# Ones as a sixteen-column denominator beside each head's values, division in the stage that follows each attention

## The chip, the cores and the metric

The kernel runs on one core of one Trainium2 chip. The metric is the device time of one execution, in microseconds (us). A core has a matrix engine (PE, with PEld for its weight loads), a vector engine (DVE), a scalar engine (ACT), a general one (POOL), and SP, which here only issues transfers (DMAs). Each engine runs its own list of instructions in order, and they wait for each other through semaphores; transfers run on 16 DMA engines.

## The reference

Eight batches of 512 tokens, 256 wide, go through a transformer layer with 16 heads of 16 columns each:

```
x = x + xattn(layernorm(x), ctx)                # 1601 context rows, 16 heads, softmax
g = layernorm(x)
h = g + causal_self_attention(rmsnorm(g)*g1)    # rotary, 16 heads of 16
y = h + moe(rmsnorm(h)*g2)                      # 8 experts, top 2
x = x + y
```

Both attentions compute, per head and query, `sum_k exp(s_k - max) v_k / sum_k exp(s_k - max)`. The change concerns only how the sum in the denominator is produced, stored and divided by.

## The kernel before, in words

`build` (from L1917) runs stages one after the other, each closed by a barrier of all engines (`Prog.clear`, L62): weights, projections of the inputs, cross attention, `invert_denominators` (L841), `project_self` (L887), self attention, `invert_denominators` again, `finish_self` (L1150), routing, experts, combination.

**attention (L442).** The work is 32 units, one for each batch and group of four heads (GH = 4). In a unit PE computes the scores of a tile of 128 keys with 512 queries (`scores`, L649), ACT takes the exponential, and PE multiplies values by probabilities into one bank `ps_o` of 128 rows (`products`, L661). Each head owns VW = 32 columns of the weights `va`: 16 values, one column of ones, 15 of zeros. So of the 32 rows of `ps_o` that a head owns, 16 are numerators, one is the denominator and 15 are zero. ACT copies the bank to `ob` (`take_out`, L808), and SP stores it (`send_out`, L587) as one transfer of 128 rows of 512 numbers, 256 KB.

SP's list in one unit u (`unit`, L591) is: wait until PE has finished the last products of unit u-1; load the values of unit u+1 (cross) or u+3 (self), in 8 or 4 transfers; load keys and queries of unit u+3 in 12 transfers (`load_kq`); wait for `take_out` of unit u-1; store it. PE first needs the keys and queries of unit u+3 at step 5 of the 16 steps of unit u+1 (self), when the row maxima for that unit begin (`in_order`, L534). POOL's part at the start of each attention is the memsets of `va`.

**invert_denominators.** SP gathers the 128 denominator rows (one for each unit and head) into a 128x512 tile, DVE takes the reciprocal, SP stores it; then a barrier.

**load_attention_out (L865).** SP loads, for one batch, the numerators in four transfers of 128 KB into `oT` (128 x 2 x 512) and the inverses in two transfers of 256 KB, each inverse row repeated over 16 partitions, into `inv`.

**project_self and finish_self.** Both work batch by batch in turns (`turns`, L137): in one turn every engine runs its parts for several batches, the lag saying how many batches behind. In `project_self` DVE's list in turn t is: `subtract_high` of k (batch t-3), `residual` (t-1), `divide` (t), `rope` of q (t-2), `layer_norm` (t-1), `rms_inverse` (t-1), `subtract_high` of q (t-2), `rope` of k (t-2). PE's is: `turn_rows` (t-1), `out_product` (t), `q_products`, `v_product`, `k_products` (t-1). The k products wait until DVE has read the q products (`rope_read`). SP's is: wait for `divide` (t-1), load batch t, then stores of k, v, rows and q. `residual` waits for the stores of the rows of the batch before (`rows_sent`). In `finish_self` DVE's list is `residual` (t-1), `divide` (t), `mean_square`, `rms_inverse`, logits; SP loads the rows of batch t-1 and the attention output of batch t.

Of the kernel before, what the change touches and what calls it, by code (L numbers as in the profile page):

```python
# [8 lines left out]
ALU = mybir.AluOpType  # L9
# [3 lines left out]
P = 128  # L13
DIM = 256
KC = DIM // P
HEADS = 16
HD = DIM // HEADS
GH = 4
# [423 lines left out]
def attention(nc, q_parts, k_parts, v_rows, out_rows, kv, causal, keep, units, beside=None):  # L442
# [28 lines left out]
    with ExitStack() as stack:  # L471
# [30 lines left out]
        KQ = 16 * 2 * PAIRS  # L502
        VLOADS = 16 * GH * ((1 if kv >= P else 0) + (1 if kv % P else 0))
# [60 lines left out]
        with nc.Block() as block:  # L564
            @block.sync
            def _(sp):
# [36 lines left out]
                for k in range(2):  # L603
                    sp.sem_inc(o_sent[k], 16)
# [11 lines left out]
                for k in range(2):  # L616
                    sp.wait_ge(o_sent[k], 16 * (units // 2 + 1))

            @block.tensor
            def _(pe):  # L620
# [71 lines left out]
                pe.wait_ge(ones_set, BUFS + 2 * VBUFS + 1)  # L692
# [43 lines left out]
            def _(pool):  # L736
# [7 lines left out]
                pool.wait_ge(ones_set, BUFS + 2 * VBUFS)  # L744
                nc.gpsimd.memset(nm_parts[:, 3:, :], 0.0).then_inc(ones_set, 1)
                pool.wait_ge(ones_set, BUFS + 2 * VBUFS + 1)
# [35 lines left out]
            def _(act):  # L782
# [25 lines left out]
                def take_out(u):  # L808
                    act.wait_ge(pv_done, (u.n + 1) * STEPS + RING)
                    act.wait_ge(o_sent[u.odd], u.loads(2) * 16)  # L810
                    nc.scalar.copy(ob[u.odd][:, :], ps_o[:, :]).then_inc(o_read, 1)
# [26 lines left out]
def invert_denominators(nc, out_rows, inverse, own, units):  # L838

    n = units * GH  # L840
    with ExitStack() as stack:  # L841
        p = Prog(nc, stack, "inv_self_" if own else "inv_cross_")
        den = p.sb("den", [n, SEQ])
        inv = p.sb("inv", [n, SEQ])
        den_in = p.sem("den_in")
        inv_ready = p.sem("inv_ready")
        inv_sent = p.sem("inv_sent")
        with nc.Block() as block:
            @block.sync
            def _(sp):  # L850
                src = out_rows.rearrange("u (j w) n -> u j w n", w=VW)[:, :, HD, :].rearrange("u j n -> (u j) n")
                sp.dma_start(den[:, :], src).then_inc(den_in, 16)
                sp.wait_ge(inv_ready, 1)
                sp.dma_start(inverse, inv[:, :]).then_inc(inv_sent, 16)
                sp.wait_ge(inv_sent, 16)

            @block.vector
            def _(dve):
                dve.wait_ge(den_in, 16)
                nc.vector.reciprocal(inv[:, :], den[:, :]).then_inc(inv_ready, 1)  # L860
        p.clear()
# [15 lines left out]
ATT_LOADS = 16 * (GROUPS + KC)  # L877

def project_self(nc, x_in, out_rows, inverse, x1_rows, h0_rows, q_parts, k_parts, v_rows, keep, batches):


    with ExitStack() as stack:
        p = Prog(nc, stack, "slf_")
        oT = p.sb("oT", [P, KC, SEQ])
        inv = p.sb("inv_rows", [P, KC, SEQ])  # L887
# [20 lines left out]
        on_ready = p.sem("on_ready")  # L908
        xb_ready = p.sem("xb_ready")
# [26 lines left out]
        with nc.Block() as block:  # L936
            @block.sync
            def _(sp):
                def load(b):
                    sp.wait_ge(on_ready, b + 1)  # L940
                    load_attention_out(sp, out_rows, inverse, oT, inv, b, att_in)
# [84 lines left out]
            def _(dve):  # L1026
# [123 lines left out]
def finish_self(nc, out_rows, inverse, x1_rows, h0_rows, y_rows, hn_rows, keep, batches):  # L1150

    logits = keep["logits"]
    with ExitStack() as stack:
        p = Prog(nc, stack, "fin_")
        oT = p.sb("oT", [P, KC, SEQ])
        inv = p.sb("inv_rows", [P, KC, SEQ])
# [14 lines left out]
        on_ready = p.sem("on_ready")  # L1171
        o_done = p.sem("o_done")
# [14 lines left out]
        with nc.Block() as block:  # L1187
            @block.sync
            def _(sp):
                def load_attention(b):  # L1190
                    sp.wait_ge(on_ready, b + 1)
                    load_attention_out(sp, out_rows, inverse, oT, inv, b, att_in)
# [41 lines left out]
            def _(dve):  # L1234
# [3 lines left out]
                def divide(b):  # L1238
                    dve.wait_ge(att_in, (b + 1) * ATT_LOADS)
                    nc.vector.tensor_tensor(on[:, :, :], oT[:, :, :], inv[:, :, :], ALU.mult).then_inc(on_ready, 1)  # L1240
# [687 lines left out]
def build(nc, a, out, batches=8):  # L1928
# [6 lines left out]
    out_rows = dram("out_rows", [units, P, SEQ])  # L1935
    inverse = dram("inverse", [units * GH, SEQ])
# [3 lines left out]
    out2_rows = dram("out2_rows", [units, P, SEQ])  # L1940
    inverse2 = dram("inverse2", [units * GH, SEQ])
# [8 lines left out]
    with ExitStack() as stack:  # L1950
# [15 lines left out]
        with ExitStack() as zeros_stack:  # L1966
            z, beside = zeros_beside(nc, in_sorted, zeros_stack, tiles, units)
            attention(nc, q_parts, k_parts, v_rows, out_rows, CTX, False, keep, units, beside)
            z.clear()
        invert_denominators(nc, out_rows, inverse, False, units)  # L1970
        project_self(nc, a["x"], out_rows, inverse, x1_rows, h0_rows, q2_parts, k2_parts, v2_rows, keep, batches)
        beside = gate_up_beside(nc, a, keep, p, units)
        attention(nc, q2_parts, k2_parts, v2_rows, out2_rows, SEQ, True, keep, units, beside)
        invert_denominators(nc, out2_rows, inverse2, True, units)
# [4 lines left out]
        finish_self(nc, out2_rows, inverse2, x1_rows, h0_rows, y_rows, hn_rows, keep, batches)  # L1979
# [32 lines left out]
```

## Time and profile before

| | us |
|---|---|
| median of 3 runs | 3300.74 (3298.10 to 3301.28) |
| the profiled execution's own time | 3297.82 |
| its span | 3296.2 |
| PE busy | 2698.5 (82%) |
| DVE busy | 1763.2 (53%) |
| ACT busy | 1458.2 (44%) |
| POOL busy | 490.7 (15%) |

Busy shares are averages over stages with different limits. The stages' places in the span, from the starts of their first instructions: cross attention to 1660, first inversion 1661 to 1670, `project_self` 1670 to 1903, self attention 1903 to 2296, second inversion 2297 to 2306, `finish_self` from 2306. In a row of the timeline the first number is the start in us from the span's start, the second the time from the start of the first instruction in the row to the end of its last, then engine (SPq and ACTq are the issuing of a DMA), line, operation, output and inputs, shapes and count, and in brackets the idle time before and what ended it.

### The profile page before, as it was taken

Reading aid. Unit: us, or ns where it says so; the run is one execution under the profiler, and the core shown is the slowest. Engines: PE = TensorE matmul, PEld = TensorE weight load, DVE = VectorE, ACT = ScalarE, POOL = GpSimd, SP = SyncE. Lnnn points to the kernel's source line nnn. Section 1 sums busy time; section 2 is a strip of 40 time slices with the busy share of each in tenths; the row PEclk is TensorE's granted clock in tenths of the full one; section 3 lists DMA queues with packets and bytes.
Section 4 is the critical chain, followed back from the end, with each engine's and each line's share of the span. In section 5 each row is a group of like instructions: output and inputs, shape, how many; then the busy total and the mean of one; then the engine's idle time right before and its main releaser. Section 6 shows DMA issues by size and latency. Waiting matters only on the chain. (4 is left out here: it accounts for less than half of the span.)

```text
span 3296.2 us, 55561 instructions
## 1 busy us (share of the span) xinstructions
PE 2698.5 (82%) x14654; PEld 1323.0 (40%) x14655; DVE 1763.2 (53%) x2832; ACT 1458.2 (44%) x2927; POOL 490.7 (15%) x650
## 2 busy tenths in 40 slices
PE   7996999999999999999949879887340299999980
PEld 5662232323232323233225434443340177777760
DVE  4565876767676767677436656664222022222223
ACT  2331576767676767677723336565010022222210
POOL 2444000000000000000014421110223300000006
PEclk9996899999999999999979979999665699999995
DMA  6777544444454444454035456653444211100116
GB/s 211 215 233 133 70 62 67 62 66 63 62 64 62 63 63 63 62 63 61 17 115 185 159 121 133 133 133 102 149 150 155 84 32 32 32 32 32 32 47 183
DMA packets 524784, 313.32 MB, mean 95 GB/s; under 512 B 312112, under 2 KB 486848, under 8 KB 524480
## 3 DMA queue, kind: packets, MB, share of 16 engines
q1 hardware_dynamic: 492752, 256.93, 38.6%
q0 software_dynamic: 11392, 37.76, 3.5%
q10 hardware_dynamic: 20464, 16.40, 1.6%
q8 instruction: 96, 1.57, 0.2%
q14 instruction: 80, 0.66, 0.1%
HBM read 188.91 MB, written 121.26 MB: 94 GB/s over the span
## 5 line engine op out<-in xcount | busy, mean ns | idle before, releaser
L719 DVE TENSOR_REDUCE att_cross_neg_max<-att_cross_ps_s 128x1 f32<-128x802 f32 x1024 | 965.6, 988 | 350.9 <-PE att_cross_ps_s L636 349.2
L794 ACT ACTIVATE att_cross_probs<-att_cross_ps_st 128x512 f32<-128x512 f32 (+1 forms) x1664 | 901.2, 599 | 394.7 <-PE att_cross_ps_st L655 382.2
L655 PE MATMUL att_cross_ps_st<-att_cross_q_pack,att_cross_k_pack 99*128 99x512 bf16 (+1 forms) x1664 | 575.0, 391 | 37.3 <-issue 28.4
L636 PE MATMUL att_cross_ps_s<-att_cross_k_pack,att_cross_q_pack 96*128 96x401 bf16 x2048 | 547.9, 350 | 70.1 <-DVE att_cross_neg_max L719 29.5
L670 PE MATMUL att_cross_ps_o<-att_cross_probs,att_cross_v_tiles 128*32 128x512 f32 (+1 forms) x3328 | 453.5, 618 | 1.0
L636 PEld LDWEIGHTS att_cross_ps_s<-att_cross_k_pack,att_cross_q_pack 96*128 96x128 bf16 x2048 | 176.8, 100 | 420.5 <-DVE att_cross_neg_max L719 204.9
L655 PEld LDWEIGHTS att_cross_ps_st<-att_cross_q_pack,att_cross_k_pack 99*128 99x128 bf16 (+1 forms) x1664 | 163.1, 100 | 415.5 <-ACT att_cross_probs L794 293.2
L719 DVE TENSOR_REDUCE att_self_neg_max<-att_self_ps_s 128x1 f32<-128x128 f32 (+3 forms) x512 | 236.2, 489 | 148.7 <-PE att_self_ps_s L639 145.7
L794 ACT ACTIVATE att_self_probs<-att_self_ps_st 128x256 f32<-128x256 f32 (+3 forms) x512 | 208.2, 441 | 142.4 <-PE att_self_ps_st L658 136.6
L1744 DVE COPY moe_hiddenT<-moe_ps_h 128x256 f32<-128x256 f32 x142 | 60.3, 425 | 296.9 <-PE moe_ps_h L1654 296.9
L636 PE MATMUL att_self_ps_s<-att_self_k_pack,att_self_q_pack 96*128 96x128 bf16 (+3 forms) x512 | 158.7, 312 | 56.4 <-DMA att_self_q_pack<-q_parts 25.1
L1708 ACT ACTIVATE moe_silu<-moe_ps_g 128x352 f32<-128x352 f32 x142 | 65.8, 463 | 301.0 <-PE moe_ps_u L1646 301.0
L1664 PE MATMUL moe_ps_y<-top_wd_sb,moe_hiddenT 128*128 (+1 forms) x852 | 196.0, 379 | 1.1 <-DVE moe_hiddenT L1745 1.1
L1646 PE MATMUL moe_ps_g<-top_wg_sb,moe_rowsT 128*128 x568 | 192.8, 462 | 0.0
L1646 PE MATMUL moe_ps_u<-top_wu_sb,moe_rowsT 128*128 x568 | 192.0, 461 | 0.0
L765 POOL CAST att_cross_neg_max_parts<-att_cross_neg_max_merged 128x16 bf16<-128x16 f32 x32 | 6.1, 192 | 1236.9 <-DVE att_cross_neg_max_merged L710 1236.9
L1664 PEld LDWEIGHTS moe_ps_y<-top_wd_sb,moe_hiddenT 128*128 128x128 f32 (+1 forms) x852 | 161.7, 190 | 35.1 <-issue 1.4
L655 PE MATMUL att_self_ps_st<-att_self_q_pack,att_self_k_pack 99*128 99x256 bf16 (+3 forms) x512 | 154.8, 304 | 7.7 <-DMA att_self_q_pack<-att_self_neg_max_rows 6.5
L1738 DVE TENSOR_TENSOR moe_hidden<-moe_ps_u,moe_silu 128x352 f32<-128x352 f32 x142 | 73.5, 517 | 159.2 <-ACT moe_silu L1708 159.2
L1816 POOL DMA_INDIRECT comb_row<-out_sorted,comb_index x64 | 61.9, 968 | 622.5 <-DVE comb_index L1826 603.3
L1646 PEld LDWEIGHTS moe_ps_u<-top_wu_sb,moe_rowsT 128*128 128x128 f32 x568 | 108.5, 191 | 60.7 <-issue 1.0
L670 PEld LDWEIGHTS att_cross_ps_o<-att_cross_probs,att_cross_v_tiles 128*32 128x32 f32 (+1 forms) x3328 | 66.6, 109 | 151.5 <-ACT att_cross_probs L794 113.8
(208 smaller groups left out, 2901.7 us busy)
## 6 DMA issues: line engine op xcount, KB each, us to landing
att_cross_k_pack<-k_parts SPq DMA_DIRECT2D x192, 200.1 KB, 7.5
k_parts<-in_part SPq DMA_DIRECT2D x72, 256.0 KB, 3.1
in_rows<-in_ctx_dram SPq DMA_DIRECT2D x24, 512.0 KB, 4.4
v_rows<-in_v_biased SPq DMA_DIRECT2D x24, 512.0 KB, 2.9
att_cross_q_pack<-q_parts SPq DMA_DIRECT2D x192, 64.0 KB, 7.7
att_cross_v_tiles<-v_rows SPq DMA_DIRECT2D x128, 96.0 KB
att_self_k_pack<-k_parts SPq DMA_DIRECT2D x192, 64.0 KB, 3.1
att_self_q_pack<-q_parts SPq DMA_DIRECT2D x192, 64.0 KB, 3.1
```

Source lines behind the costliest of these rows:

```text
L636: last = nc.tensor.matmul(ps_s[bank][:, n, 0:w], qp[v.buf][0:SROWS, j, q * P:(q + 1) * P], kp[v.buf][0:SROWS, j, s:s + w], start=True, sto ...
L655: mm = nc.tensor.matmul(ps_st[bank_of_step[s]][0:rows, q0:SEQ], kp[u.buf][0:MROWS, j, t * P:t * P + rows], qp[u.buf][0:MROWS, j, q0:SEQ], ...
L670: nc.tensor.matmul(ps_o[j * VW:(j + 1) * VW, q0:SEQ], va[u.vbuf][0:rows, t, j, :], pr[0:rows, (u.odd * STEPS + t * GH + j) % RING, q0:SEQ] ...
L719: nc.vector.tensor_reduce(nmax[v.odd][:, col, half:half + 1], ps_s[bank][:, 0:len(spans), 0:spans[0][1]], AX.XY, ALU.max, negate=True).the ...
L765: link(nc.gpsimd.tensor_copy(nm_parts[:, 0, :], full))
L794: nc.scalar.activation(pr[0:rows, (u.odd * STEPS + s) % RING, q0:SEQ], ps_st[bank_of_step[s]][0:rows, q0:SEQ], ACT.Exp).then_inc(exp_done, 1)
L1646: last = nc.tensor.matmul(ps[half][:, 0:HHALF], xT[t.par][:, i, :], wt[:, bass.ds(at, HHALF)], start=(i == 0), stop=(i == KC - 1))
L1664: last = nc.tensor.matmul(ps_y[:, :], hT[half][0:CW[c], c, :], wd[0:CW[c], bass.ds(at, DIM)], start=(half == 0 and c == 0), stop=(half == ...
L1708: nc.scalar.activation(sil[half][:, :], ps_g[half][:, 0:HHALF], ACT.Silu).then_inc(sil_ready, 1)
L1738: nc.vector.tensor_tensor(h[half][:, :], ps_u[half][:, 0:HHALF], sil[half][:, :], ALU.mult)\
L1744: nc.vector.tensor_copy(hT[half][:, 0:CH - 1, :], ps_h[half][:, 0:CH - 1, :])
L1816: pool.indirect_dma_start(out=r[g][k][c][:, :], out_offset=None, in_=out_sorted, in_offset=bass.IndirectOffsetOnAxis(ap=index[g][:, c, k:k ...
```

## The change

`va` gets 16 columns of ones instead of one of ones and 15 of zeros, so each head owns 16 numerator rows and 16 equal denominator rows. `send_out` stores them in eight transfers of 16 rows (32 KB) instead of one of 128 rows (256 KB): four to `out_rows` and four to `den_rows`, both now [batch, 256, 512]. Both calls of `invert_denominators` and the stage itself are gone. `load_attention_out` loads one batch with two transfers of 512 KB. `divide` in both stages takes the reciprocal of the whole 128x1024 tile of denominators in place, waits for it, and multiplies.

```diff
 def send_out(v):
     sp.wait_ge(o_read, v.n + 2)
-    sp.dma_start(out_rows[v.n, :, :], ob[v.odd][:, :]).then_inc(o_sent[v.odd], 16)
+    for rows, first in ((out_rows, 0), (den_rows, HD)):
+        for j in range(GH):
+            sp.dma_start(rows[v.batch, v.rows.start + j * HD:v.rows.start + (j + 1) * HD, :],
+                         ob[v.odd][j * VW + first:j * VW + first + HD, :]).then_inc(o_sent[v.odd], 16)
...
 for k in range(VBUFS):
-    nc.gpsimd.memset(va[k][:, :, :, HD + 1:VW], 0.0).then_inc(ones_set, 1)
-    nc.gpsimd.memset(va[k][:, :, :, HD:HD + 1], 1.0).then_inc(ones_set, 1)
+    nc.gpsimd.memset(va[k][:, :, :, HD:VW], 1.0).then_inc(ones_set, 1)
...
-def load_attention_out(eng, out_rows, inverse, oT, inv, b, arrived):
-
-    for c in range(KC):
-        for u in range(GROUPS // KC):
-            src = out_rows[b * GROUPS + (c * (GROUPS // KC) + u), :, :].rearrange("(j w) n -> j w n", w=VW)
-            eng.dma_start(oT[u * GR:(u + 1) * GR, c, :], src[:, 0:HD, :]).then_inc(arrived, 16)
-        heads = HEADS // KC
-        src = inverse[bass.ds(b * HEADS + c * heads, heads), :].unsqueeze(1).broadcast_to([heads, HD, SEQ])
-        eng.dma_start(inv[:, c, :], src).then_inc(arrived, 16)
+def load_attention_out(eng, out_rows, den_rows, oT, den, b, arrived):
+
+    for src, dst in ((out_rows, oT), (den_rows, den)):
+        eng.dma_start(dst[:, :, :], src[b, :, :].rearrange("(c p) n -> p c n", p=P)).then_inc(arrived, 16)
...
 def divide(b):
     dve.wait_ge(att_in, (b + 1) * ATT_LOADS)
-    nc.vector.tensor_tensor(on[:, :, :], oT[:, :, :], inv[:, :, :], ALU.mult).then_inc(on_ready, 1)
+    nc.vector.reciprocal(den[:, :, :], den[:, :, :]).then_inc(inverted, 1)
+    dve.wait_ge(inverted, b + 1)
+    nc.vector.tensor_tensor(on[:, :, :], oT[:, :, :], den[:, :, :], ALU.mult).then_inc(on_ready, 1)
...
-invert_denominators(nc, out_rows, inverse, False, units)
...
-invert_denominators(nc, out2_rows, inverse2, True, units)
```

SP's list in one self attention unit, from the last loads of keys and queries over the store of the output to the values of the next unit (ISA and REGISTER_ALU rows are address and wait instructions). Before:

```order
L572 DMA att_self_q_pack<-q_parts 16x4x512
L588 REGISTER_ALU
L589 ISA [waits att_self_o_read]
L589 DMA out_rows<-att_self_out_buf 128x512
L594 ISA
L580 ISA [waits att_self_pv_done]
L580 DMA att_self_v_tiles<-v_rows 128x4x16
```

And now:

```order
L573 DMA att_self_q_pack<-q_parts 16x4x512
L589 REGISTER_ALU
L592 ISA [waits att_self_o_read]
L592 DMA out_rows<-att_self_out_buf 16x512
L592 ISA
L592 DMA out_rows<-att_self_out_buf 16x512
L592 ISA
L592 DMA out_rows<-att_self_out_buf 16x512
L592 ISA
L592 DMA out_rows<-att_self_out_buf 16x512
L592 DMA den_rows<-att_self_out_buf 16x512 x4
L598 ISA
```

Seven more transfers stand between the queries of one unit and the values of the next.

DVE's list in one turn of `project_self`, from the moments of the residual to the q rope. Before:

```order
L176 BN_AGGR slf_norm_mean_var<-slf_norm_stats 128x2 x4
L1031 REGISTER_ALU
L1032 TENSOR_TENSOR slf_o_normed<-slf_oT,slf_inv_rows 128x1024 [waits slf_att_in]
L1059 ISA
L1060 REGISTER_ALU [waits slf_rope_done]
L1062 TENSOR_TENSOR slf_rope_cos<-slf_ps_a,top_keep_constants 128x512 [waits slf_full_ready0]
```

And now:

```order
L176 BN_AGGR slf_norm_mean_var<-slf_norm_stats 128x2 x4
L1002 REGISTER_ALU
L1003 RECIPROCAL slf_denominators<-slf_denominators 128x1024 [waits slf_att_in]
L1005 TENSOR_TENSOR slf_o_normed<-slf_oT,slf_denominators 128x1024 [waits slf_inverted]
L1032 ISA
L1033 REGISTER_ALU [waits slf_rope_done]
L1035 TENSOR_TENSOR slf_rope_cos<-slf_ps_a,top_keep_constants 128x512 [waits slf_full_ready0]
```

A reciprocal of 1024 columns stands ahead of the multiplication, and with it ahead of everything that DVE does later in the turn.

## Rows read from the trace of the kernel before

**Rows 1.** Windows: length, busy us (count) PE, PEld, DVE, ACT, POOL; clock, DMA, GB/s.
```profile
1700.00:1860.00 160.00, 148.11 (x491) 88.88 (x492) 107.99 (x240) 54.92 (x87) 73.07 (x49) 0.98 0.54 177
1934.00:2292.00 358.00, 322.34 (x3021) 154.85 (x3017) 220.72 (x479) 219.14 (x567) 42.25 (x154) 1.00 0.57 128
2305.00:2460.00 155.00, 65.05 (x272) 54.73 (x272) 38.77 (x97) 21.14 (x42) 35.17 (x31) 0.66 0.48 153
```

**Rows 2.** Timeline from the first inversion stage to the first division of project_self.
```profile
1660.96 0.34 SPq L852 DMA_DIRECT2D inv_cross_den<-out_rows  x1
1663.63 3.35 DVE L860 RECIPROCAL inv_cross_inv<-inv_cross_den 128x512 f32<-128x512 f32 x1 [50.27 <-DMA inv_cross_den<-out_rows]
...
1670.02 1.30 SPq L871 DMA_DIRECT2D slf_oT<-out_rows  x2
...
1681.54 1.22 DVE L1032 TENSOR_TENSOR slf_o_normed<-slf_oT,slf_inv_rows 128x1024 f32<-128x1024 f32 x1 [14.56 <-DMA slf_inv_rows<-inverse]
```

**Rows 3.** Instructions on one tile: L1044, duration ns min/median/max.
```profile
L1044 DVE RECIPROCAL slf_norm_std_inv<-slf_norm_std x8: 159/168/171, 1695.5 to 1858.3; 128x4 f32<-128x4 f32 x8
```

**Rows 4.** DMA issues of the page: count, KB each, median us to landing.
```profile
fin_x<-x_rows SPq DMA_DIRECT2D x8, 512.0 KB, 4.6
fin_h<-h_rows SPq DMA_DIRECT2D x8, 512.0 KB, 6.8
```

**Rows 5.** Timeline of DVE and PE in project_self, turns 1 to 3.
```profile
1694.32 1.23 DVE L1032 TENSOR_TENSOR slf_o_normed<-slf_oT,slf_inv_rows 128x1024 f32<-128x1024 f32 x1 [2.82 <-DMA slf_inv_rows<-inverse]
...
1712.31 1.22 DVE L1038 TENSOR_TENSOR slf_x<-slf_ps_o,slf_x_biased 128x1024 f32<-128x1024 f32 x1 [10.37 <-DMA h_rows<-slf_h]
...
1734.13 1.23 DVE L1070 TENSOR_TENSOR slf_roped_rest<-slf_roped,slf_roped_part 128x1024 f32<-128x1024 f32 x1 [4.59 <-ACT slf_roped_part L1113]
...
1738.36 1.19 DVE L1032 TENSOR_TENSOR slf_o_normed<-slf_oT,slf_inv_rows 128x1024 f32<-128x1024 f32 x1
...
1745.76 3.60 PE L1003 MATMUL slf_ps_b<-slf_xT,top_keep_wk_rot 128*128 128x512 f32 x8
...
1750.60 1.09 PE L994 MATMUL slf_ps_t<-top_keep_constants,slf_x_rms 128*128 128x128 f32 x8 [1.25 <-ACT slf_x_rms L1095]
```

**Rows 6.** Clock: a window of finish_self, and sixteen equal matmuls in project_self (timeline).
```profile
2321.00:2327.00 6.00, 5.48 (x16) 4.18 (x16) 0.42 (x2) 0.00 (x0) 0.00 (x0) 0.69 0.27 84
...
1728.55 3.62 PE L985 MATMUL slf_ps_o<-top_keep_WoT,slf_o_normed 128*128 128x256 f32 x16
```

**Rows 7.** Timeline of SP and PE in two self attention units; landing of the queries.
```profile
2057.94 2.09 SPq L580 DMA_DIRECT2D att_self_v_tiles<-v_rows  x4
2060.22 0.35 SPq L569 DMA_DIRECT2D att_self_k_pack<-k_parts  x1
...
2065.70 0.38 SPq L572 DMA_DIRECT2D att_self_q_pack<-q_parts  x1
...
2069.19 2.06 SPq L580 DMA_DIRECT2D att_self_v_tiles<-v_rows  x4
...
2069.58 0.22 PE L636 MATMUL att_self_ps_s<-att_self_k_pack,att_self_q_pack 96*128 96x128 bf16 x1
...
att_self_q_pack<-q_parts SPq DMA_DIRECT2D x192, 64.0 KB, 3.1
```

**Rows 8.** SP's waits in the two attentions: us in total, times, longest us.
```profile
SPq L580 <- PE att_self_ps_o L670: 65.3, 28, 8.0
...
SPq L580 <- PE att_cross_ps_o L670: 907.2, 30, 43.2
```

**Rows 9.** Timeline: the second inversion stage and the first load of finish_self.
```profile
2296.82 0.35 SPq L852 DMA_DIRECT2D inv_self_den<-out_rows  x1
...
2305.66 1.28 SPq L871 DMA_DIRECT2D fin_oT<-out_rows  x2
```

**Rows 10.** Timeline: first and last of the eight divisions in finish_self.
```profile
2319.79 1.22 DVE L1240 TENSOR_TENSOR fin_o_normed<-fin_oT,fin_inv_rows 128x1024 f32<-128x1024 f32 x1 [17.00 <-DMA fin_inv_rows<-inverse]
...
2445.78 1.23 DVE L1240 TENSOR_TENSOR fin_o_normed<-fin_oT,fin_inv_rows 128x1024 f32<-128x1024 f32 x1 [5.94 <-DMA fin_inv_rows<-inverse]
```

More of the change, by code:

```diff
@@ L438, in project_inputs, with attention @@
         p.clear()
-def attention(nc, q_parts, k_parts, v_rows, out_rows, kv, causal, keep, units, beside=None):
+def attention(nc, q_parts, k_parts, v_rows, out_rows, den_rows, kv, causal, keep, units, beside=None):
     tiles = [(t, min(P, kv - t * P)) for t in range(-(-kv // P))]
@@ L616, in _ @@
                 for k in range(2):
-                    sp.wait_ge(o_sent[k], 16 * (units // 2 + 1))
+                    sp.wait_ge(o_sent[k], OSENT * (units // 2 + 1))
             @block.tensor
@@ L809, in take_out @@
                     act.wait_ge(pv_done, (u.n + 1) * STEPS + RING)
-                    act.wait_ge(o_sent[u.odd], u.loads(2) * 16)
+                    act.wait_ge(o_sent[u.odd], u.loads(2) * OSENT)
                     nc.scalar.copy(ob[u.odd][:, :], ps_o[:, :]).then_inc(o_read, 1)
@@ L834, in attention, with project_self @@
         p.clear()
[L838 to L861, printed above, removed]
-def load_attention_out(eng, out_rows, inverse, oT, inv, b, arrived):
-    for c in range(KC):
-        for u in range(GROUPS // KC):
-            src = out_rows[b * GROUPS + (c * (GROUPS // KC) + u), :, :].rearrange("(j w) n -> j w n", w=VW)
-            eng.dma_start(oT[u * GR:(u + 1) * GR, c, :], src[:, 0:HD, :]).then_inc(arrived, 16)
-        heads = HEADS // KC
-        src = inverse[bass.ds(b * HEADS + c * heads, heads), :].unsqueeze(1).broadcast_to([heads, HD, SEQ])
-        eng.dma_start(inv[:, c, :], src).then_inc(arrived, 16)
-ATT_LOADS = 16 * (GROUPS + KC)
-def project_self(nc, x_in, out_rows, inverse, x1_rows, h0_rows, q_parts, k_parts, v_rows, keep, batches):
+def load_attention_out(eng, out_rows, den_rows, oT, den, b, arrived):
+    for src, dst in ((out_rows, oT), (den_rows, den)):
+        eng.dma_start(dst[:, :, :], src[b, :, :].rearrange("(c p) n -> p c n", p=P)).then_inc(arrived, 16)
+ATT_LOADS = 16 * 2
+def project_self(nc, x_in, out_rows, den_rows, x1_rows, h0_rows, q_parts, k_parts, v_rows, keep, batches):
     with ExitStack() as stack:
@@ L1146, in project_self, with finish_self @@
         p.clear()
-def finish_self(nc, out_rows, inverse, x1_rows, h0_rows, y_rows, hn_rows, keep, batches):
+def finish_self(nc, out_rows, den_rows, x1_rows, h0_rows, y_rows, hn_rows, keep, batches):
     logits = keep["logits"]
@@ L1934, in build @@
     v_rows = dram("v_rows", [batches, CTX, DIM])
-    out_rows = dram("out_rows", [units, P, SEQ])
-    inverse = dram("inverse", [units * GH, SEQ])
+    out_rows = dram("out_rows", [batches, DIM, SEQ])
+    den_rows = dram("den_rows", [batches, DIM, SEQ])
     k2_parts = dram("k2_parts", [batches, 3, DIM, SEQ], BF16)
@@ L1939, in build @@
     v2_rows = dram("v2_rows", [batches, SEQ, DIM])
-    out2_rows = dram("out2_rows", [units, P, SEQ])
-    inverse2 = dram("inverse2", [units * GH, SEQ])
+    out2_rows = dram("out2_rows", [batches, DIM, SEQ])
+    den2_rows = dram("den2_rows", [batches, DIM, SEQ])
     tokens = batches * SEQ
@@ L1967, in build @@
             z, beside = zeros_beside(nc, in_sorted, zeros_stack, tiles, units)
-            attention(nc, q_parts, k_parts, v_rows, out_rows, CTX, False, keep, units, beside)
+            attention(nc, q_parts, k_parts, v_rows, out_rows, den_rows, CTX, False, keep, units, beside)
             z.clear()
-        invert_denominators(nc, out_rows, inverse, False, units)
-        project_self(nc, a["x"], out_rows, inverse, x1_rows, h0_rows, q2_parts, k2_parts, v2_rows, keep, batches)
+        project_self(nc, a["x"], out_rows, den_rows, x1_rows, h0_rows, q2_parts, k2_parts, v2_rows, keep, batches)
         beside = gate_up_beside(nc, a, keep, p, units)
-        attention(nc, q2_parts, k2_parts, v2_rows, out2_rows, SEQ, True, keep, units, beside)
-        invert_denominators(nc, out2_rows, inverse2, True, units)
+        attention(nc, q2_parts, k2_parts, v2_rows, out2_rows, den2_rows, SEQ, True, keep, units, beside)
         keep["logits"] = p.sb("logits", [P, tokens // P, EXPERTS])
@@ L1978, in build @@
         keep["tile_expert"] = p.sb("tile_expert", [P, tiles], I32)
-        finish_self(nc, out2_rows, inverse2, x1_rows, h0_rows, y_rows, hn_rows, keep, batches)
+        finish_self(nc, out2_rows, den2_rows, x1_rows, h0_rows, y_rows, hn_rows, keep, batches)
         route(nc, keep, tokens)
```

23 lines of the change are left out of this document (14 added, 9 removed).

## The prediction

> **What bounds the kernel now.** I read the windows first, cut at the stages that the change touches. In `project_self` PE is busy 148 of 160 us and DVE 108; in self attention PE 322 of 358; in `finish_self` nobody is busy for half the time [rows 1]. A busy share doesn't say whether an added microsecond shows, so in each stage I look for the wait that ends last.
>
> In `project_self` that is a ring through DVE's list. In a steady turn DVE starts `subtract_high` of k at 1734.13 after waiting 4.59 us for ACT, which waited for POOL, which waited for what DVE did at the end of the turn before. From there DVE runs residual, moments, division (1738.36), rope, layer norm without a gap [rows 5]. PE's k products wait for the rope of q, end at 1749.36 (1745.76 + 3.60), and 1.24 us later `turn_rows` begins, waiting for ACT's scaled rows, again from DVE [rows 5]. Whatever is put between residual and rope lengthens the ring. In self attention PE sets the pace, but SP is close behind: it waits for PE only 65.3 us in 28 units, 2.33 us in each [rows 8]. In `finish_self` the division waits for its loads in every turn [rows 10].
>
> **What is removed.** The two inversion stages: 1660.96 to 1670.02, or 9.06 us, and 2296.82 to 2305.66, or 8.84 us [rows 2, 9]. Both lie bare between barriers, so both go in full.
>
> **Price of a reciprocal.** 128x512 took 3.352 us (3.35 in [rows 2]) and 128x4 0.168 us [rows 3]: 6.27 ns a column, 0.14 us fixed. For 1024 columns 6.56 us. Doubling the first row gives 6.70, the 1.19 us of a 1024-column multiplication [rows 5] is the floor; I take 6.56, since it follows the operation's own two sizes. There are now 8 of them in each stage.
>
> **Price of the stores.** Each unit has seven more issues on SP. Twelve key and query issues of 32 or 64 KB start from 2060.22 to 2065.70, 0.50 us apart [rows 7]; the four value issues take 2.09 us. Seven at 0.50 us are 3.5 us a unit. The lower end is 7 x 0.35 (an issue's own duration), 2.5 us, the upper 7 x 0.56 (the values' spacing), 3.9 us.
>
> **Cross attention: nothing.** SP waits 907.2 us there [rows 8], more than 28 us a unit, and covers 3.5. Values of one instead of zero leave the matmuls' shapes alone, and the memsets get fewer. If this cover were gone it would be 32 x 3.5 us; nothing suggests it.
>
> **End of cross attention to the first division.** The last store is bare: +3.5. The inversion goes: -9.06. The load took 11.52 us from first issue to division (1670.02 to 1681.54) [rows 2]. The new one is two transfers of 512 KB; a pair of that size and form lands 6.8 us after the second is issued, some 7.4 after the first [rows 4]. The same bytes in the old form give 11.52 as the upper end; I take 7.4, the row of the same shape: -4.1. The reciprocal is bare: +6.56. Together -3.1.
> The Trainium skill, on its page "DMA: Bandwidth & Descriptors" (section "Why a DMA increments its semaphore by 16 and not by 1"), says that a transfer is split over the largest number of engines, up to 16, that divides the outermost dimension on both sides. By that the old numerator loads (outermost 4) would use 4 of 16 engines and the new ones all; if it didn't hold, the loads would take their old times and the sum would be 4.1 + 6.7 + 7 x 5.4 = 49 us higher.
>
> **project_self, turn 1.** The division had waited 2.82 us for its load [rows 5]; it waits no more, so the reciprocal costs 6.56 - 2.8 = +3.8. The residual of the next turn waited 10.37 us for the rows' store [rows 5], queued behind the loads that get 4 us shorter, and PE's product was ready about 2.5 us before it: of 3.8, +1.3 is left.
>
> **project_self, turns 2 to 7.** Each takes 6.56 in full, since DVE has no gap between residual and rope and the ring closes through both rope and layer norm. The steady residual waits up to 0.58 us for the stores, 0.3 on average, which vanishes. The k products can now start only about 6 us after the v products end, so PE stands idle once a turn. After such a gap the granted clock in `finish_self` is 0.69 on average, between the 1.2 GHz level and the 2.4 GHz one, and 16 matmuls take 5.48 us, where they take 3.62 in `project_self` at 2.4 GHz [rows 6]: 1.9 us more for a burst, of which 1.24 is slack, so +0.6. A turn costs 6.56 - 0.3 + 0.6 = 6.9; six turns +41.4. The stage with its boundary comes to -3.1 + 1.3 + 41.4 = **+39.6**.
>
> **Self attention.** SP's unit gets 3.5 us longer and has 2.33 us to give [rows 8]. Is there a reserve in how early it loads? The last queries of a unit are issued at 2065.70 and land 3.1 us later, at 2068.8; PE uses them at 2069.58 [rows 7]. So 0.8 us, once. From the second or third unit on PE waits for keys and queries, and the unit's period becomes SP's: 3.5 - 2.33 = 1.17 us longer. Over 27 units **+31.6**. With 2.5 us for the issues it is about +4, with 3.9 about +42. What is queued behind SP's issues are the very loads that PE waits for; ACT's `take_out` waits for a store two units old and is not reached first.
>
> **Second boundary.** +3.5 for the last store, -8.84, load 14.13 (2305.66 to 2319.79 [rows 9, 10]) to 7.4: -6.7, reciprocal +6.56. Together **-5.5**.
>
> **finish_self, turns 1 to 7.** Divisions are 126.0 us apart over seven turns, 18.0 each [rows 10]. Each waits for its load, and the next load is issued when it is done, so a shorter load pays and the reciprocal costs. The two first loads took 11.5 and 14.1 us, 12.8 on average; against 7.4 that saves 5.4. 6.56 - 5.4 = 1.2 a turn, **+8.4**. The ends are -0.1 (saving of 6.7) and 6.56 (no saving): -1 to +46.
>
> **Sum.** 39.6 + 31.6 - 5.5 + 8.4 = +74.1. The profiled execution took 3297.8 us, so 3371.9; the median of the runs shown lies 2.9 higher, which gives **3375 us**.
>
> **Rivals.**
> A. *SP keeps up.* The issues go out at their own duration, and PE hardly waits: self attention costs some 4 us instead of 32. 3375 - 28 = 3347. For it: issue rows of 0.35 to 0.38 us; against it: in steady loops the starts are 0.50 apart. Chance 15%.
> B. *The final stage pays for each reciprocal.* The load's speed is not what ends its turn, because transfers of other tensors hold it: +46 instead of +8, 3413. For it: other loads and stores share each turn; against it: those transfers can use the reciprocal's time. Chance 11%.
> C. *The clock.* After the idle gap the k products, 7.2 us at 2.4 GHz, run wholly at 1.2 GHz: 7.2 more, less 1.24 of slack, 6.0 instead of 0.6 in six turns, +32, 3407. For it: that gap is new in every turn. Against it: after idle stretches in `finish_self` a burst lost 1.9 us, not its whole length [rows 6]. Chance 4%.
> The Trainium skill's page "TensorE: Matmul & The Clock Gate" (section "HAM oscillation — how this bites in real kernels") has the rule behind this: a wait in every tile drops the clock each time, and the next tile starts slow. The windows agree as far as 0.69 against 1.00 goes.
> D. *Faster.* The reciprocals vanish in DVE's idle time, and the removed stages are a net gain. In `project_self` DVE is idle 52 us of 160 [rows 1] and eight reciprocals are 52.5 us; `finish_self` has 116 idle. Then the sum is -9.06 - 8.84 + 7.0 - 4.1 - 6.7 = -21.7, 3279, provided SP keeps up too. It decides if a turn of `project_self` is set by PE alone, with DVE's 4.59 us wait being true slack. Against it: that wait is the ring's own. Chance 4%.
> The other 66% are the forecast.
>
> **How the numbers follow.** The range takes the bounds of the stores' price (3347 to 3386), and reaches up to B and C: 3340 to 3415. Below it lie D and the cheaper half of A, above it B and C with dear stores; about 2 in 10. A measurement can tell 0.2%, 6.6 us, from no change. Faster is D, 0.04; A together with free reloads in the final stage could come near zero only if `project_self` paid little, 0.02; slower 0.94.
>
> **What would show it.** `project_self`: turns of 30 us instead of 23.4, an idle PE of some 6 us before the k products, reciprocals of 6.5 to 6.6 us. Self attention: waits of PE for DMA of keys and queries, SP's wait for PE near zero, units of 12.3 us. `finish_self`: first division near 15 us after the first issue, turns near 19. No inversion rows. It is wrong if SP still waits 2 us a unit, if turns of `project_self` grow by less than 5 us, or if loads of 512 KB land as slowly as the old ones.

## The result, and the profile after

The median after the change is **3332.49 us** (4 runs, 3329.0 to 3333.01) against 3300.15 us before (4 runs of the same comparison): a ratio of 1.0096, 95% interval 1.0079 to 1.0114, so 1% slower. The profiled execution took 3329.0 us, its span is 3327.4 us (before 3296.2): 31.2 us more. The forecast was 74 us more, and 3332.49 lies below the range of 3340 to 3415: the direction was right, the size wrong.

Cut at the same instructions, the two spans compare so. The stages are: `project_self` from its first attention load to the first key load of self attention; self attention from there to the last `take_out`; then the boundary to the first load of `finish_self`; `finish_self` to the first memset of routing.

| us | before | after | difference | forecast |
|---|---|---|---|---|
| first load of `project_self` at | 1670.0 | 1664.3 | -5.7 | -5.6 |
| `project_self` | 233.6 | 276.5 | +42.9 | +45.2 |
| self attention | 388.6 | 416.0 | +27.4 | +31.6 |
| second boundary | 13.5 | 7.9 | -5.6 | -5.3 |
| `finish_self` | 177.1 | 151.1 | **-25.9** | **+8.3** |
| the rest of the program | 813.5 | 811.6 | -1.9 | 0 |

Five lines hold within 5 us. One has the wrong sign, and it alone makes up 34 of the 43 us by which the forecast was off.

The end of the first boundary and the first division of `project_self` after the change (timeline; answers to [rows 2]):

```profile
1658.27 1.81 SPq L592 DMA_DIRECT2D den_rows<-att_cross_out_buf  x4
...
1664.27 0.40 SPq L844 DMA_DIRECT2D slf_oT<-out_rows  x1
1664.72 0.46 SPq L844 DMA_DIRECT2D slf_denominators<-den_rows  x1
...
1669.33 6.55 DVE L1003 RECIPROCAL slf_denominators<-slf_denominators 128x1024 f32<-128x1024 f32 x1 [56.13 <-DMA slf_denominators<-den_rows]
```

No inversion stands there, and the reciprocal takes 6.55 us as priced from the 128x512 and the 128x4 one (6.56). But the load is there 5.06 us after its first issue (before 11.52, forecast 7.4). One steady turn of `project_self` (timeline of DVE and PE, turns 4 and 5; answers to [rows 5]):

```profile
1770.13 6.52 DVE L1003 RECIPROCAL slf_denominators<-slf_denominators 128x1024 f32<-128x1024 f32 x1
1770.71 3.62 PE L988 MATMUL slf_ps_t<-top_keep_wv,slf_xT 128*128 128x256 f32 x16
...
1780.36 5.95 PE L974 MATMUL slf_ps_a<-slf_xT,top_keep_wk 128*128 128x512 f32 x8 [6.03 <-DVE slf_rope_sin L1036]
...
1786.14 3.60 PE L974 MATMUL slf_ps_b<-slf_xT,top_keep_wk_rot 128*128 128x512 f32 x8
...
1789.58 1.04 PE L965 MATMUL slf_ps_t<-top_keep_constants,slf_x_rms 128*128 128x128 f32 x8
...
1795.96 1.23 DVE L1043 TENSOR_TENSOR slf_roped_rest<-slf_roped,slf_roped_part 128x1024 f32<-128x1024 f32 x1 [3.70 <-ACT slf_roped_part L1086]
...
1800.18 6.52 DVE L1003 RECIPROCAL slf_denominators<-slf_denominators 128x1024 f32<-128x1024 f32 x1
```

The turn is 30.05 us (1770.13 to 1800.18), with DVE's 3.70 us wait for ACT still in it, so the ring is the one of before with a link more. PE stands idle 6.03 us before the k products, and the first eight of them take 5.95 us instead of 3.60.

SP in a self attention unit, and the waits of the stage from its first unit on (timeline, then waits: who for whom, us in total, times, longest; answers to [rows 7, 8]):

```profile
2105.01 1.88 SPq L592 DMA_DIRECT2D out_rows<-att_self_out_buf  x4
2106.98 1.76 SPq L592 DMA_DIRECT2D den_rows<-att_self_out_buf  x4
2109.02 2.22 SPq L581 DMA_DIRECT2D att_self_v_tiles<-v_rows  x4
...
SPq L581 <- PE att_self_ps_o L674: 8.1, 1, 8.1
...
PE att_self_ps_s L640 <- DMA att_self_q_pack<-q_parts: 30.4, 22, 2.8
```

The next unit's value loads start at 2121.39, 12.37 us after these: SP issues without a pause. It waits for PE once, where it waited 28 times, and PE now waits for queries 22 times, 30.4 us in all.

The first turns of `finish_self` after the change, the last division, and its transfers (timeline, then DMA issues with us to landing; answers to [rows 9, 10, 4]):

```profile
2364.68 0.41 SPq L844 DMA_DIRECT2D fin_oT<-out_rows  x1
...
2370.00 6.55 DVE L1214 RECIPROCAL fin_denominators<-fin_denominators 128x1024 f32<-128x1024 f32 x1 [27.16 <-DMA fin_denominators<-den_rows]
...
2392.78 5.25 PE L1184 MATMUL fin_ps_o<-top_keep_wo,fin_o_normed 128*128 128x256 f32 x16 [9.04 <-DVE fin_o_normed L1216]
...
2398.06 1.23 DVE L1223 TENSOR_TENSOR fin_h<-fin_ps_o,fin_h 128x1024 f32<-128x1024 f32 x1 [2.54 <-PE fin_ps_o L1184]
2399.20 6.54 DVE L1214 RECIPROCAL fin_denominators<-fin_denominators 128x1024 f32<-128x1024 f32 x1
...
2477.76 6.55 DVE L1214 RECIPROCAL fin_denominators<-fin_denominators 128x1024 f32<-128x1024 f32 x1
...
fin_oT<-out_rows SPq DMA_DIRECT2D x8, 512.0 KB, 4.2
fin_denominators<-den_rows SPq DMA_DIRECT2D x8, 512.0 KB, 5.1
hn_rows<-fin_h_normed ACTq DMA_DIRECT2D x8, 512.0 KB, 4.8
```

The first load takes 5.3 us (before 14.1). The later ones are there 5.3 to 7.4 us after their first issue, and DVE comes for them 6.3 to 7.9 us after it: of the later reciprocals only the seventh waits for its load, 0.90 us. A turn is (2477.76 - 2370.00) / 7 = 15.4 us, where it was 18.0 and 19.2 was forecast. The store of the normalised rows lands after 4.8 us, before after 8.9, though nothing of that store was edited.

So the questions are: do the eight stores make self attention longer, and through SP (E1)? What does a reciprocal cost in each stage (E2, E3)? What makes the loads fast (E4, E5, E7, E9)? What holds a turn of `finish_self` (E10, E11)?

### The profile page after: what moved, and what is told of

The parts are those of the page before. It is cut to its first block and busy times, and to the rows that moved or that the text cites. A ratio compares the mean times of both kernels' runs of the same rounds, so it can differ in the third digit from the quotient of the medians.

```text
span 3327.4 us, 56360 instructions
## 1 busy us (share of the span) xinstructions
PE 2721.3 (82%) x14654; PEld 1331.6 (40%) x14655; DVE 1860.1 (56%) x2846; ACT 1461.7 (44%) x2927; POOL 486.7 (15%) x644
```

## The experiments

Times of stages are read as in the table above. A time without an interval is that of one execution, to be compared with the 3329.0 us of the change's profiled one. The runs were taken in four groups, each with the kernel before beside it, and its median differed from group to group: 3300.15 us beside the change, 3303.07 beside E1 to E4, 3293.07 beside E5 and E7 to E9, 3300.92 beside E10 and E11. What lies behind `finish_self`, which no edit touches, took 811.6 to 813.6 us in the first two groups, 805.2 to 808.2 in the third, 814.6 to 814.9 in the fourth. So whole times of two groups can lie up to 10 us apart without any edit, and the argument goes by the stages.

### E1. One store instead of eight

```diff
-    for rows, first in ((out_rows, 0), (den_rows, HD)):
-        for j in range(GH): ...
+    sp.dma_start(out_rows[v.n, :, :], ob[v.odd][:, :]).then_inc(o_sent[v.odd], 16)
...
+    src = out_rows[bass.ds(b * GROUPS + c * 2, 2), :, :]
+    src = src.rearrange("u (j w) n -> (u j) w n", w=VW)[:, first:first + HD, :]
+    eng.dma_start(dst[:, c, :], src).then_inc(arrived, 16)
```

> One store of 128 rows a unit again instead of eight of 16, and the loads in four transfers of 256 KB (8 heads of 16 rows each) because the rows lie as before. Theory (SP's issues delay the loads of keys and queries): the self attention stage falls from 416.6 us back to 389, its unit from 12.37 to 11.1, SP waits over 2 us a unit again; each boundary loses 3 us. Span 3327 - 27 - 6 = 3294, up to 10 more if four loads land later than two. Rival (the denominator rows' extra lines or the memory written, not the number of issues, slow the stage): self attention stays at 416, span about 3321.

Self attention fell from 416.0 to 391.9 us, and SP waits for PE as before the change (waits of E1):

```profile
SPq L581 <- PE att_self_ps_o L671: 69.8, 28, 8.3
```

So the seven added issues are what lengthens self attention: 24 of the 27 us go with them. It isn't the memory written, for E1 writes the same 256 KB in a unit. Yet the whole took 3335.21 us (2 runs; ratio 1.0098, interval 1.0069 to 1.0127), no better than the change, because the loads that have to pick their rows out of the mixed store are slow again. First load of `finish_self` (timeline of E1):

```profile
2340.65 1.38 SPq L844 DMA_DIRECT2D fin_oT<-out_rows  x2
2342.09 1.24 SPq L844 DMA_DIRECT2D fin_denominators<-out_rows  x2
...
2350.90 6.55 DVE L1214 RECIPROCAL fin_denominators<-fin_denominators 128x1024 f32<-128x1024 f32 x1 [28.55 <-DMA fin_denominators<-out_rows]
```

10.2 us instead of 5.3; the turn is 19.0 us and `finish_self` 180.3. I had expected the form of these four loads to cost little and a span of 3294 to 3304 us; it was 3334.6.

### E2 and E3. No reciprocal in one of the stages

```diff
 def divide(b):
     dve.wait_ge(att_in, (b + 1) * ATT_LOADS)
-    nc.vector.reciprocal(den[:, :, :], den[:, :, :]).then_inc(inverted, 1)
-    dve.wait_ge(inverted, b + 1)
     nc.vector.tensor_tensor(on[:, :, :], oT[:, :, :], den[:, :, :], ALU.mult).then_inc(on_ready, 1)
```

E2 leaves this out in `project_self`, E3 in `finish_self`; each multiplies by the denominators there instead of dividing by them.

> The changed kernel without the reciprocal in project_self (it multiplies by the denominators; what it computes is not the reference). Theory (the reciprocal lies bare in DVE's ring, and the idle gap of PE costs some 0.5 us a turn): turns fall from 30.0 to 23.3, the first division comes 6.5 us earlier, stage -50, span 3277. Rival (the ring grew for another reason, such as the denser loads colliding with stores): turns stay above 25, span above 3290.

> The changed kernel without the reciprocal in finish_self (not the reference's computation). Theory (a turn of 15.4 us is product, residual, reciprocal, multiplication in a row, with the load of 5 us hidden beside product and residual): the turn falls until the chain of stores and loads over two turns sets it, 11 to 12 us; with the first reciprocal -34, span 3293. If nothing else binds, 8.5 us a turn and span 3273. Rival (a turn is set by the transfers' total of 3 MB): turn stays above 14, span above 3310.

E2 took 3278.2 us: `project_self` 276.5 to 223.1, 53.4 us for eight reciprocals of 6.55 us, 52.4 in all. The stage pays for them in full, though not evenly: the seven turns get 3.9 to 7.6 us shorter. Its steady turn is 22.96 us (multiplications at 1746.58 and 1769.55), against 30.05 and more, so with the colder k products a reciprocal costs 7.1 us in a steady turn.

E3 took 3320.3 us: `finish_self` 151.1 to 142.0, only 9.1 us for the same 52.4. The divisions, eight of them from 2370.2 to 2469.7, lie 14.2 us apart, just 1.2 less than with the reciprocal. I had expected 11 to 12 us and a span of 3293; the rival noted there, a turn above 14 us and a span above 3310, came true, and E10 below shows what holds that turn. What fills the rest of the turn there (timeline of E3, fourth and fifth turn):

```profile
2418.60 1.22 DVE L1220 TENSOR_TENSOR fin_h<-fin_ps_o,fin_h 128x1024 f32<-128x1024 f32 x1 [10.27 <-DMA fin_h<-h_rows]
...
2422.08 1.77 DVE L1213 TENSOR_TENSOR fin_o_normed<-fin_oT,fin_denominators 128x1024 f32<-128x1024 f32 x1 [2.26 <-DMA fin_denominators<-den_rows]
```

Without the reciprocal DVE waits for transfers of other tensors. SP too issues the next attention load late, 3.6 to 7.5 us after the multiplication in five of seven turns, because its loads of rows stand first and wait for POOL. With the reciprocal that time passes under it: SP then issues 0.16 to 0.27 us after every multiplication.

### E4 and E5. The form of the loads

E4 is E1 with the numerators and denominators loaded in the old form, eight transfers of 128 KB with four heads outermost. E5 keeps the dense stores and loads them in eight transfers of 128 KB too, but with 32 rows outermost.

```diff
 E4:
+    src = out_rows[b * GROUPS + c * 2 + u, :, :].rearrange("(j w) n -> j w n", w=VW)
+    eng.dma_start(dst[u * GR:(u + 1) * GR, c, :], src[:, first:first + HD, :]).then_inc(arrived, 16)
 E5:
+    for i in range(4):
+        eng.dma_start(dst[i * 32:(i + 1) * 32, :, :],
+                      src[b, :, :].rearrange("(c p) n -> p c n", p=P)[i * 32:(i + 1) * 32, :, :]).then_inc(arrived, 16)
```

> One store a unit as in the run with one store, and the loads in the old form: eight transfers of 128 KB whose source has four heads as its outermost dimension. Theory (the form makes the old loads slow, since few DMA engines serve one): the first load of finish_self takes 11 to 14 us instead of 5.3, the turn 20 to 22 instead of 15.4; self attention 389; span 3294 + 8 + 50 = about 3350. Rival (bytes and total traffic decide, not the form): first load near 6 to 8, turn 16 to 17, span below 3310.

> The changed kernel with each load of a batch cut into four pieces of 32 partitions: eight transfers of 128 KB, as many and as large as in the run with the old form (first load of finish_self 15.4 us, stage 222 us), but 32 as their outermost dimension instead of 4. Theory (the form, through the number of engines that serve a transfer): first load 7 to 8 us, 5.3 plus the longer issue; finish_self from first load to routing 151 to 158 us, span 3328 to 3338. Rival (number and size of the transfers): first load near 15 us, stage near 222, span near 3398.

First loads of `finish_self` (timeline of E4, then of E5):

```profile
2358.23 2.43 SPq L844 DMA_DIRECT2D fin_oT<-out_rows  x4
2360.70 2.34 SPq L844 DMA_DIRECT2D fin_denominators<-out_rows  x4
...
2373.65 6.55 DVE L1214 RECIPROCAL fin_denominators<-fin_denominators 128x1024 f32<-128x1024 f32 x1 [33.74 <-DMA fin_denominators<-out_rows]
```

```profile
2367.50 1.75 SPq L845 DMA_DIRECT2D fin_oT<-out_rows  x4
2369.29 1.84 SPq L845 DMA_DIRECT2D fin_denominators<-den_rows  x4
...
2373.93 6.55 DVE L1217 RECIPROCAL fin_denominators<-fin_denominators 128x1024 f32<-128x1024 f32 x1 [27.75 <-DMA fin_denominators<-den_rows]
```

The same 1 MB in the same number of transfers: 15.4 us in the one form, 6.4 in the other. E4 took 3395.4 us, with 303.5 us in `project_self` and 222.1 in `finish_self`, where a turn is 24.2 us; that is dearer than I had expected. E5 took 3338.5 us; against the change `finish_self` is 10.0 us longer (161.2) and `project_self` 2.9. So number and size of the transfers cost something, 16.8 us a turn instead of 15.4, but they are not what makes the old loads slow. E4 and E5 differ in the stores as well; E1 and E9 below have the same store and four loads of 256 KB each, with 8 and with 16 outermost, and take 10.2 and 6.9 us.

### E7. The kernel before, with sixteen outermost

If that is so, the kernel before can have fast loads without new stores, inversions kept: numerators and inverses are loaded with the 16 columns of a head outermost. The rows of `oT` then come in another order (column, then head), so the rows of both output weights are permuted once to fit.

```diff
-        for u in range(GROUPS // KC): ...
+        src = out_rows[bass.ds(b * GROUPS + c * (GROUPS // KC), GROUPS // KC), :, :]
+        src = src.rearrange("u (j w) n -> w (u j) n", w=VW)[0:HD, :, :]
+        eng.dma_start(oT[:, c, :], src).then_inc(arrived, 16)
...
-        src = inverse[...].unsqueeze(1).broadcast_to([heads, HD, SEQ])
+        src = inverse[...].unsqueeze(0).broadcast_to([HD, heads, SEQ])
```

> The kernel before, inversion stages and single store kept, but the order of a head's rows and the heads is swapped within a chunk of 128 (Wo's rows follow), so that each of the four loads of a batch, 256 KB, has 16 as outermost dimension. Theory (faster loads alone are worth 10 us in project_self and 35 us in finish_self, which the changed kernel had and lost again to the reciprocals and stores): stages 223 and 142 us, span 3296 - 45 = 3251. Rival (the gain in finish_self came with the denser order of the whole change, not with the loads): finish_self stays above 165 us, span above 3280.

3251.67 us median of 4 runs, ratio to the kernel before 0.9871 (0.9854 to 0.9887): 1.3% faster. `finish_self` takes 143.1 us instead of 177.1, self attention 387.3 and `project_self` 227.0. First load of `finish_self` (timeline of E7):

```profile
2300.37 0.63 SPq L885 DMA_DIRECT2D fin_oT<-out_rows  x1
...
2307.28 1.23 DVE L1254 TENSOR_TENSOR fin_o_normed<-fin_oT,fin_inv_rows 128x1024 f32<-128x1024 f32 x1 [10.21 <-DMA fin_inv_rows<-inverse]
```

6.9 us instead of 14.1. The turn is (2405.2 - 2307.3) / 7 = 14.0 us instead of 18.0. So 4.0 us a turn is what fast loads give by themselves, with no reciprocal in the stage and no other store of the attention in play.

### E8. The reciprocal at another place of DVE's turn

```diff
-turns(dve, batches, ((3, lambda b: subtract_high(1, b)), (1, residual), (0, divide), ...
+turns(dve, batches, ((0, invert), (3, lambda b: subtract_high(1, b)), (1, residual), (0, divide), ...
```

The reciprocal of `project_self` is put at the start of the turn, where DVE waited for ACT; `divide` keeps the multiplication.

> The changed kernel with the reciprocal of project_self as the first item of DVE's turn, ahead of the wait for ACT, the multiplication left in its place. Theory (the reciprocal is bare only where it stands; DVE has 4.9 us of waiting at the start of a turn): a turn falls from 27.4 on average, 30.4 steady, by 4 to 5 us, and so does each of some six turns: project_self 276 to 250, span 3302. Rival (DVE's total work, or PE's clock after an idle gap, sets the turn): less than 10 us in all, span above 3317.

`project_self` 276.5 to 245.4 us, and 3293.2 us in all, beside 3293.07 of the kernel before in the same group. Reciprocals in its steady turns (timeline of E8):

```profile
1752.31 6.54 DVE L1003 RECIPROCAL slf_denominators<-slf_denominators 128x1024 f32<-128x1024 f32 x1
...
1776.73 6.54 DVE L1003 RECIPROCAL slf_denominators<-slf_denominators 128x1024 f32<-128x1024 f32 x1
```

24.4 us a turn: against 22.96 without any (E2) the reciprocal costs 1.5 us here and 7.1 where the change has it. The duration is the same; its place decides. I had expected 26 us of gain, it was 31.

### E9. One store, sixteen outermost, reciprocals in the stages

E1 with the loads of E7.

> The changed computation (sixteen ones, reciprocal in the two stages) with one store a unit and loads of 256 KB with 16 as outermost dimension, through the swapped order of rows. Theory: self attention 390 us instead of 416, both boundaries 3 us shorter, first load 5.5 to 6.5 us, finish_self 151 to 153, project_self 276: span 3327 - 25 - 6 + 1 = 3297. Rival (four transfers cannot land as fast as two): first load above 8, finish_self above 165, span above 3312.

3308.0 us: 28 less than E1, 21 less than the change, of which 7 and 5 us lie behind `finish_self`, where the groups differ. Self attention 393.4, `finish_self` 162.3 us; I had expected 151 to 153 for the latter. The load is there 6.9 us after its first issue (timeline of E9), 1.6 us later than in the change, and the turn is 16.7 us instead of 15.4. The trace ties the two: five of E9's seven later reciprocals wait for their load, 7.3 us in all, where the change has one such wait of 0.90:

```profile
2337.55 1.27 SPq L858 DMA_DIRECT2D fin_oT<-out_rows  x2
...
2344.43 6.55 DVE L1228 RECIPROCAL fin_denominators<-fin_denominators 128x1024 f32<-128x1024 f32 x1 [25.12 <-DMA fin_denominators<-out_rows]
```

### E10 and E11. The store of the normalised rows first in ACT's turn

In `finish_self` POOL may write the next normalised rows only once the last ones are stored, and ACT issued that store last in its turn. Both kernels issue it first; E10 is E7 with that edit, E11 is the change with it.

```diff
-turns(act, batches, ((2, take_turned), (0, root_mean_square), (0, scale_rows), (0, store_y), (1, store_normed)))
+turns(act, batches, ((1, store_normed), (2, take_turned), (0, root_mean_square), (0, scale_rows), (0, store_y)))
```

> The run with sixteen-engine loads and kept inversion stages, with ACT storing the normalised rows of finish_self at the head of its turn instead of the end. Theory (with the reciprocal gone, the turn of 14.0 us is held by the chain store of these rows, POOL's two operations, the next loads, over two turns): the store is issued 2 to 4 us earlier after POOL's result, the turn falls to 12 to 13, finish_self 143 to 130 to 138, span 3237 to 3245. Rival (3 MB of transfers a turn hold it): turn stays at 14, span within 3 of 3250.

> The same edit on the changed kernel. Theory (there the turn of 15.4 us is DVE's and PE's own ring: product, residual, reciprocal, multiplication, with every transfer hidden): nothing changes, turn 15.2 to 15.5, span 3325 to 3329. Rival (the same chain of stores holds the turn there too): turn down by 1 us or more, span below 3321.

POOL's wait for that store in `finish_self` (waits of E7, then of the change):

```profile
POOL fin_h_normed L1330 <- DMA hn_rows<-fin_h_normed: 70.9, 7, 13.0
```

```profile
POOL fin_h_normed L1292 <- DMA hn_rows<-fin_h_normed: 71.6, 7, 12.9
```

In E10 and in E11 these waits are gone. In E10 the turn falls from 14.0 to 12.0 us and the stage from 143.1 to 123.0; in E11 nothing moves (turn 15.3, stage 150.4 us, 3332.1 us in all), and POOL waits 68.6 us for ACT's rows instead. The same 71 us of waiting were the end of the turn in the one kernel and slack in the other, where DVE's reciprocal and PE's product set it.

Set side by side, the two spans show only 8 of E10's 20 us (3242.0 against 3250.1), but they come from two groups. Against the kernel before of its own group E7 is 41.4 us faster and E10 58.4, so some 17 of the 20 us arrive. Behind `finish_self` E7 has 806.6 us and E10 814.9, each like the other kernels of its group. Self attention takes 3.7 us longer in E10, and no run says why. The median of E10 is 3242.49 us (4 runs, ratio to the kernel before 0.9818, 0.9802 to 0.9835), the fastest version of the case, 1.8% below the kernel before.

## Why the prediction was wrong

**The step that failed: "`finish_self`, turns 1 to 7", 18.0 - 5.4 + 6.56 = 19.2 us.** Measured, it is 18.0 - 4.0 (E7) + 1.4 = 15.4. The load's saving was put 1.4 us too high; the reciprocal was put at its whole duration and costs 1.2 (against E3) to 1.4. The premise was that a division waits for its load, the next load is issued when it is done, and so the turn is load plus DVE's time.

Already in the kernel before that holds for five turns of seven only. In the other two SP issued the load 5.7 and 6.4 us after the multiplication, since its loads of rows stand first and wait for POOL's result (timeline of before):

```profile
2364.84 1.76 DVE L1240 TENSOR_TENSOR fin_o_normed<-fin_oT,fin_inv_rows 128x1024 f32<-128x1024 f32 x1 [9.57 <-DMA fin_inv_rows<-inverse]
2368.51 2.35 POOL L1309 TENSOR_TENSOR fin_y<-fin_x,fin_h 128x1024 f32<-128x1024 f32 x1
2371.05 0.38 SPq L1197 DMA_DIRECT2D fin_x<-x_rows  x1
2372.31 1.64 SPq L871 DMA_DIRECT2D fin_oT<-out_rows  x2
```

From first issue to division the seven loads took 11.1 to 19.6 us, 14.7 on average, not the 12.8 of the two first loads. In E7 that average falls by 5.3 us, close to the 5.4 of the sum, but SP issues another 1.0 us later a turn, so 4.0 are left.

In the change the load no longer comes last at all: it lands within the product and the residual, which fill the 6.3 to 7.9 us from its issue to the next reciprocal, and it drops out of the sum. The turn is then the longer of two rings. One is DVE and PE alone: reciprocal 6.5, multiplication 1.2 to 2.2, product 5.3 to 6.6, residual 1.2, which makes 14.3 to 16.0 us. The other is the transfers with POOL and ACT, 14.2 without the reciprocal. The reciprocal lies beside the second ring, not on top of it. The product in the first ring took 3.62 us in `project_self` at 2.4 GHz; here, with a mean granted clock of 0.68 from 2370 to 2485 us, it takes 1.6 to 3.0 more, which the sum had no term for.

Summed over the stage, E3 against the change: +6.6 for the first reciprocal, which is bare, +8.3 in seven turns, and -5.7 after the last division, where the other ring has caught up; 9.1 in all, where the forecast had set eight times 6.56 in full. Of the 34 us by which the forecast missed the stage, 26 lie in the seven turns, 2 in the first load and 5.5 after the last division, a stretch for which the sum had nothing.

Rival B asked whether the load's speed is really what ends the turn, because transfers of other tensors hold it. It was right that they do, and drew the wrong side from it: if something else holds the turn at 14 us, it covers an added operation just as it covers a saved wait. The prediction's own word against B, that those transfers can use the reciprocal's time, is what happened; the sum of 19.2 us did not use it.

**A smaller miss: the first loads.** 7.4 us was read from a pair that is issued behind the attention's own loads. First in line, two such transfers took 5.1 and 5.3 us: 2.3 us in `project_self`, 2.1 in `finish_self`.

**First boundary, inversions, reciprocal's duration:** -5.7 against -5.6; 6.52 to 6.55 us against 6.56. Right.

**project_self:** turns of 29.3 to 30.6 us against a forecast of 30, from the third on; E2 shows 53.4 us for eight reciprocals. That the stage's sum came within 2.3 us is in part luck: the first turn grew by 4.5 us where 1.3 was forecast, the second by 3.7 where 6.9 was, and these two misses cancel. The argument (no gap in DVE's list between residual and rope, a ring that closes through both) stands, and E8 confirms it from the other side: moved to the wait in the same list, the same instruction costs 1.5 us. Rival D, that idle DVE time takes it in, falls for the change's order and nearly holds for E8's.

**Self attention:** +27.4 against +31.6, E1 takes 24 back. The unit is 12.37 us against the 12.3 forecast. Rival A, that SP keeps up, falls.

**The clock:** PE stands idle for 6.0 to 6.1 us before the k products of every steady turn, and their first group then takes longer than its 3.60 us: 5.30, 5.95, 6.28 and 6.45 us in four turns in a row. Those turns last 29.41, 30.05, 30.39 and 30.55 us, so they grow in step with the burst. Taking off E2's 22.96 and a reciprocal of 6.55, the clock costs nothing in the first of them and 0.5 to 1.0 us in the others, where the sum had 0.6; some 1.8 us of each burst's excess are absorbed, where the sum had 1.24. The sum's 1.9 for a burst came from one in `finish_self` that followed 29.0 us of idle PE, not 6, so that it fits is partly chance. The mean granted clock over four of the turns (window of the change; columns as in [rows 1]) lies between the 1.2 GHz level and the 2.4 GHz one; in the kernel before, and in E2 and E8, it is 1.00 over the same window:

```profile
1741.00:1861.00 120.00, 95.84 (x288) 54.92 (x287) 94.15 (x147) 33.99 (x52) 46.71 (x32) 0.89 0.47 157
```

Rival C would have had 6 us a turn; it falls.

**The split of a transfer:** the rule that the prediction cites from the Trainium skill, on its page "DMA: Bandwidth & Descriptors" (section "Why a DMA increments its semaphore by 16 and not by 1"), stood beside the expectation that the loads get shorter. The runs agree with it (table at the end) and show more than the forecast took from it: the old loads' form is worth 1.3% of the kernel before (E7), and dense stores from SP were a dear way to mend it.

## What to carry to other kernels

When a wait at the end of a turn is shortened, ask what comes last next, and add new work to that ring, not to the old sum; work put beside a ring that is already as long is nearly free, and the same instruction in a list without gaps is paid in full. Look at the outermost dimension of every transfer that something waits for, on both sides, and make it a multiple of 16 by the order of the loops or of the rows, before changing what is stored. A store split into small pieces is paid at its issuing engine: seven more issues in a unit of 11 us made SP the bound.

## What the runs showed of the hardware that was not expected

The same 1 MB from first issue to first use, in the first load of `finish_self`, against the outermost dimension of the transfers:

| outermost | transfers | us | run |
|---|---|---|---|
| 4 | 8 of 128 KB | 15.4 | E4 |
| 8 | 4 of 256 KB | 10.2 | E1 |
| 16 | 4 of 256 KB | 6.9 | E9 |
| 32 | 8 of 128 KB | 6.4 | E5 |
| 128 | 2 of 512 KB | 5.3 | the change |

Below 16 the time grows as the dimension shrinks, by 3.3 us from 16 to 8 with nothing else changed but the order of the rows (E9, E1). From 16 on 1.6 us are left, in which number and size of the transfers differ too. The Trainium skill, on its page "DMA: Bandwidth & Descriptors" (section "Why a DMA increments its semaphore by 16 and not by 1"), lets a transfer run on the largest number of engines up to 16 that divides the outermost dimension of both sides: 4, 8, 16, 16 and 16 here, and these times agree.

How soon a transfer lands depended on what else was under way. The store of the normalised rows, 512 KB and the same in these kernels, lands after 11.7, 8.8, 7.1, 6.0 and 4.8 us with the loads of E4, E1, E9, E5 and the change, in the order of their speed (DMA issues of E4; those of the change are shown above):

```profile
hn_rows<-fin_h_normed ACTq DMA_DIRECT2D x8, 512.0 KB, 11.7
```

It isn't the loads' form alone. With the change's own loads the store takes 8.0 us in E3, where only the reciprocal is gone, and 2.9 us in E11, where only its place in ACT's turn is another. What is under way beside it when it is issued counts as well, and no run takes the two apart.
